# A fused layer norm, attention and token-mixing block on Trainium2: the normalised input is turned by VectorE and DMAs in place of TensorE

## The reference

```python
xn = _layernorm(x)                       # x: (8, 1024, 256), fp32
# attention: 8 query heads of 128, one shared key and value head
q  = (xn @ Wq + bq) + pe                 # Wq: (256, 1024)
k, v = split(xn @ Wkv + bkv);  k = k + pe
attn = softmax(causal(q @ k.T / sqrt(128))) @ v
attn = attn @ Wo
# token mixing
xr = mu_r * xn + (1 - mu_r) * xn_prev;   xk = mu_k * xn + (1 - mu_k) * xn_prev
ffn = sigmoid(xr @ W_r.T) * (relu(xk @ W_k.T) ** 2 @ W_v.T)
out = x + attn + ffn
```

## Time and profile before

| | us |
|---|---|
| median of 3 runs | 1504.16 (1502.83 to 1504.8) |
| the profiled execution, its own time | 1506.69 |
| its span | 1504.9 |
| PE busy | 1482.6 (99%) |
| PE weight loads busy | 1448.2 (96%) |
| DVE busy | 1268.4 (84%) |
| POOL busy | 1128.9 (75%) |
| ACT busy | 1068.0 (71%) |
| share of the chain that ended last: PE, DVE, issue, POOL | 81%, 10%, 4%, 3% |

### The profile page before, as it was taken

One profiled execution on the slowest core, in us unless ns is written; L12 is line 12 of the kernel. 1 busy time (PEld: TensorE's weight loads), 2 busy tenths in 40 slices (PEclk: granted clock), 3 DMA queues, 4 the chain that ended last, 5 costly groups with the idle time before them and its releaser, 6 DMA issues.

```text
span 1504.9 us, 36254 instructions
## 1 busy us (share of the span) xinstructions
PE 1482.6 (99%) x11724; PEld 1448.2 (96%) x11724; DVE 1268.4 (84%) x3424; ACT 1068.0 (71%) x2563; POOL 1128.9 (75%) x1541
## 2 busy tenths in 40 slices
PE   7999999999999999999999999999999999999998
PEld 7999999999999999999999999999999999999998
DVE  6999878898788987998879888798977888789885
ACT  6777667776677767767677776776767777677764
POOL 6687777777777877777777776777777787777875
PEclk8999999999999999999999999999999999999999
DMA  4144422444224442244423444134441344403453
GB/s 129 48 131 129 142 75 64 134 125 147 72 65 133 135 134 68 83 120 137 134 60 88 127 128 144 46 98 128 134 141 34 113 131 138 136 27 108 119 157 105
DMA packets 225801, 164.39 MB, mean 109 GB/s; under 512 B 51792, under 2 KB 220880, under 8 KB 225616
## 3 DMA queue, kind: packets, MB, share of 16 engines
q1 hardware_dynamic: 224768, 161.69, 35.6%
q10 hardware_dynamic: 848, 0.40, 0.1%
HBM read 81.27 MB, written 77.59 MB: 106 GB/s over the span
## 4 chain that ended last, share of the span: by engine, by line
PE 81%; DVE 10%; issue 4%; POOL 3%; DMA 1%; ACT 1%; SPq 0%; DVEq 0%; POOLq 0%; ACTq 0%
PE pS L1040 27%; PE pO L1181 22%; PE pG L1040 13%; PE pG L1127 9%; PE pT L1143 8%; DVE X L1019 2%; DVE pt L943 1%; DVE Y L923 1%; DVE kt L831 1%; POOL X L571 1%; DVE xn L808 1%; DMA park_dram<-Y 1%; DVE mix L860 1%; POOL qt L527 1%; DVE qtmp L849 1%
## 5 line engine op out<-in xcount | busy, mean ns | idle before, releaser
L764 ACT ACTIVATE X<-X,bias 128x16 f32<-128x16 f32 (+56 forms) x512 | 376.1, 734 | 150.7 <-DVE bias L1019 149.0
L1040 PE MATMUL pS<-kt,qt 128*128 128x288 f32 (+41 forms) x2304 | 460.1, 329 | 4.5 <-DVE bias L1019 3.4
L571 POOL TENSOR_SCALAR X<-X,rec 128x16 f32<-128x16 f32 (+56 forms) x512 | 378.2, 739 | 44.2 <-DVE rec L913 33.4
L1040 PEld LDWEIGHTS pS<-kt,qt 128*128 128x128 f32 x2304 | 365.7, 189 | 17.1 <-issue 5.3
L546 POOL TENSOR_TENSOR pt<-pt 128x256 fp32r<-128x256 f32 (+5 forms) x192 | 316.6, 1649 | 60.3 <-ACT pt L686 59.8
L1181 PE MATMUL pO<-pt,v 128*128 128x256 f32 x2192 | 307.6, 284 | 1.2 <-DVE ot L998 0.9
L1019 DVE CUSTOM_DVE_ANT_1 X<-pS,mask 128x528 f32<-128x528 f32 (+31 forms) x256 | 245.6, 959 | 47.1 <-PE pS L1040 42.3
L1181 PEld LDWEIGHTS pO<-pt,v 128*128 128x128 f32 x2192 | 271.9, 189 | 2.6 <-DVE ot L998 2.1
L943 DVE TENSOR_TENSOR pt<-pt,pT 128x512 fp32r<-128x512 f32 (+3 forms) x440 | 207.6, 493 | 35.1 <-ACT pt L692 32.2
L757 ACT CAST ot<-pO 128x256 fp32r<-128x256 f32 x256 | 95.5, 373 | 184.0 <-PE pO L1181 117.8
L692 ACT CAST pt<-pT 128x512 fp32r<-128x512 f32 (+3 forms) x448 | 188.0, 450 | 30.8 <-PE pT L1143 30.5
(11 more groups left out here) (120 smaller groups left out, 2298.6 us busy)
## 6 DMA issues: line engine op xcount, KB each, us to landing
park_dram<-Y SPq DMA_DIRECT2D x32, 512.0 KB, 2.6
pt<-park_dram SPq DMA_DIRECT2D x128, 128.0 KB, 2.8
park_dram<-Y SPq DMA_DIRECT2D x32, 448.0 KB, 3.0
pt<-park_dram SPq DMA_DIRECT2D x128, 112.0 KB, 2.5
park_dram<-Y SPq DMA_DIRECT2D x32, 384.0 KB, 2.9
pt<-park_dram SPq DMA_DIRECT2D x128, 96.0 KB, 2.3
park_dram<-Y SPq DMA_DIRECT2D x32, 320.0 KB, 2.7
pt<-park_dram SPq DMA_DIRECT2D x128, 80.0 KB, 2.1
```

The costliest lines, as they stand in the source:

```text
L571: nc.gpsimd.tensor_scalar(x_row(s, 0, w), x_row(s, 0, w), rec[:, j:j + 1], sign(s), ALU.mult, ALU.mult).then_inc(normed, 1)
L764: nc.scalar.activation(x_row(s, 0, w), x_row(s, 0, w), ACT.Exp, bias=bias[:, j:j + 1], scale=-1.0, accum_out=total[:, j:j + 1]).then_inc(e ...
L1040: last = nc.tensor.matmul(out, a[i], m[j], start=start and k == 0, stop=stop and k == n - 1)
```

## The change

Chunks 2 to 31 no longer go through the PE transposes of XT. DVE transposes the 32 x 32 squares of `xn` into `ka` (`turn_x`; `ka` is otherwise the activations' buffer and free at that time), SP parks `ka` in a fifth part of the DRAM buffer (`park_x`, one DMA of 256 KB) and fetches it back into `xn` with the squares in their places (`fetch_x`, four DMAs of 64 KB). ACT's two copies then read `xn` in SBUF in place of PSUM. The FK filler's activation waits until `ka` is parked (`x_parked`), `norm_apply` waits for ACT's copies (`xnt_ready`) in place of PE. `xn` is laid out by feature tile first. `MODE` becomes '0111' for rows 2 and 3: the first pair of each goes by PE. All lags, `TURNS`, `WO_AT`, `AT` and one entry of `HALVES` have new values.

```diff
--- before.py
+++ after.py
@@ -20,11 +20,11 @@
 T_LAG = 6
 PV_LAG = 8
 V_LAG = 3
-F_LAG = ((5, 2), (6, 5), (5, 5), (5, 5), (5, 6), (4, 3), (5, 5), (5, 7))
-H_LAG = ((6, 7), (9, 7), (7, 7), (7, 6), (7, 7), (7, 6), (7, 7), (7, 9))
-L_LAG = ((5, 6), (6, 7), (7, 7), (7, 9), (8, 9), (8, 11), (7, 7), (7, 8))
-W_LAG = ((7, 6), (8, 7), (7, 9), (8, 6), (7, 4), (7, 7), (7, 8), (8, 9))
-MODE = ('0000', '0000', '1111', '1111', '1111', '1111', '1111', '1111')
+F_LAG = ((4, 2), (6, 5), (5, 5), (5, 7), (4, 7), (4, 3), (5, 5), (4, 6))
+H_LAG = ((7, 7), (10, 8), (7, 8), (7, 6), (7, 9), (7, 7), (7, 7), (7, 9))
+L_LAG = ((5, 6), (7, 8), (7, 8), (8, 9), (8, 8), (7, 9), (7, 6), (7, 8))
+W_LAG = ((8, 5), (11, 5), (7, 7), (9, 6), (7, 3), (7, 5), (7, 7), (8, 9))
+MODE = ('0000', '0000', '0111', '0111', '1111', '1111', '1111', '1111')
 SCALED = ()
 C_LAG = 2
 QTMP = 4
@@ -36,10 +36,10 @@
 SHARED = NT // 2 * H
 
 
-TURNS = (((0, 'FK', 0, 0), (1, 'XT', 1, 0), (4, 'Q', 1, 0), (6, 'Q', 1, 1), (8, 'FR', 0, 0), (10, 'KV', 1, 0), (12, 'Q', 1, 2), (12, 'KT', 1, 0), (13, 'Q', 1, 3), (14, 'FV', 0, 0)), ((0, 'FK', 0, 0), (3, 'XT', 1, 0), (4, 'FR', 0, 0), (6, 'KV', 1, 0), (7, 'Q', 1, 0), (8, 'Q', 1, 1), (12, 'Q', 1, 2), (12, 'Q', 1, 3), (14, 'KT', 1, 0), (14, 'FV', 0, 0)), ((0, 'FK', 0, 0), (2, 'XT', 1, 0), (4, 'Q', 1, 0), (6, 'KV', 1, 0), (7, 'FR', 0, 0), (10, 'Q', 1, 1), (11, 'FV', 0, 0), (12, 'Q', 1, 2), (13, 'Q', 1, 3), (14, 'KT', 1, 0)), ((0, 'FK', 0, 0), (2, 'XT', 1, 0), (4, 'Q', 1, 0), (5, 'Q', 1, 1), (6, 'KV', 1, 0), (11, 'FR', 0, 0), (12, 'Q', 1, 2), (13, 'FV', 0, 0), (14, 'Q', 1, 3), (15, 'KT', 1, 0)))
-WO_AT = (17, 25, 33, 41, 49, 57, 66, 73)
-AT = {'stats': (-14, -8, -9, -7), 'apply': (-2, -1, 0, 0), 'inv': (-7, -8, -5, -6), 'mixr_prev': (0, 0, 0, 0), 'mixr_dve': (0, 0, 1, 0), 'mixr_out': (2, 1, 4, 1), 'ka_out': (4, 7, 7, 9), 'mixk_prev': (4, 8, 6, 6), 'mixk_dve': (5, 10, 6, 10), 'mixk_out': (10, 12, 10, 12)}
-HALVES = (1, 7, 6, 9, 8, 5, 1, 7, 6, 9, 8, 5, 1, 7, 6, 9, 8, 5, 1, 7, 8, 9, 1, 5, 8, 7, 1, 9, 4, 6, 5, 8, 0, 2, 4, 6, 0, 8, 4, 2, 0, 6, 4, 8, 0, 2, 4, 6, 0, 8, 4, 2, 0, 6, 4, 8, 0, 2, 4, 6, 0, 8, 4, 2)
+TURNS = (((0, 'FK', 0, 0), (1, 'XT', 1, 0), (4, 'Q', 1, 0), (5, 'Q', 1, 1), (6, 'FR', 0, 0), (12, 'Q', 1, 2), (12, 'KV', 1, 0), (12, 'Q', 1, 3), (14, 'FV', 0, 0), (15, 'KT', 1, 0)), ((0, 'FK', 0, 0), (2, 'XT', 1, 0), (4, 'FR', 0, 0), (5, 'KV', 1, 0), (7, 'Q', 1, 0), (8, 'Q', 1, 1), (12, 'Q', 1, 2), (12, 'KT', 1, 0), (14, 'Q', 1, 3), (15, 'FV', 0, 0)), ((0, 'FK', 0, 0), (2, 'XT', 1, 0), (4, 'KV', 1, 0), (6, 'FR', 0, 0), (7, 'Q', 1, 0), (10, 'Q', 1, 1), (11, 'FV', 0, 0), (12, 'Q', 1, 2), (13, 'Q', 1, 3), (14, 'KT', 1, 0)), ((0, 'FK', 0, 0), (2, 'XT', 1, 0), (4, 'Q', 1, 0), (5, 'Q', 1, 1), (6, 'Q', 1, 2), (9, 'FR', 0, 0), (10, 'KV', 1, 0), (13, 'Q', 1, 3), (15, 'FV', 0, 0), (15, 'KT', 1, 0)))
+WO_AT = (17, 26, 33, 41, 49, 56, 66, 73)
+AT = {'stats': (-14, -8, -8, -8), 'apply': (-7, -6, -7, -7), 'inv': (-9, -7, -8, -7), 'mixr_prev': (0, 0, 0, 0), 'mixr_dve': (0, 0, 1, 0), 'mixr_out': (2, 1, 4, 1), 'ka_out': (4, 6, 9, 8), 'mixk_prev': (4, 8, 6, 7), 'mixk_dve': (5, 10, 6, 9), 'mixk_out': (11, 12, 10, 14), 'xturn': (-6, -4, -5, -5), 'xfetch': (-1, -2, -3, -2)}
+HALVES = (1, 7, 6, 9, 8, 5, 1, 7, 6, 9, 8, 5, 1, 7, 6, 9, 8, 5, 1, 7, 4, 9, 1, 5, 8, 7, 1, 9, 4, 6, 5, 8, 0, 2, 4, 6, 0, 8, 4, 2, 0, 6, 4, 8, 0, 2, 4, 6, 0, 8, 4, 2, 0, 6, 4, 8, 0, 2, 4, 6, 0, 8, 4, 2)
 def fillers():
     at = {it: [] for it in range(LAST_IT)}
     for r in range(NT):
@@ -141,6 +141,11 @@
     return [1] if AT[kind][0] < 0 else []
 
 
+def by_dma(n):
+
+    return n >= 2
+
+
 def absent(b, c):
 
     return c == NC and b == B - 1
@@ -158,7 +163,8 @@
     for b, it in turns():
         if it >= T_LAG and it - T_LAG < STEPS:
             order += [(b, ("T", it - T_LAG, m)) for m in range(len(t_banks(it - T_LAG)))]
-        order += [(b, u) for u in FILL[it] if not absent(b, u[1])]
+        order += [(b, u) for u in FILL[it]
+                  if not absent(b, u[1]) and not (u[0] == "XT" and by_dma(b * NC + u[1]))]
         if SHARED <= it < STEPS:
             order.append((b, ("S", it, 0)))
     last, before = {}, {}
@@ -242,7 +248,7 @@
         mix = sb("mix", [P, CT, CHUNK])
         ka = sb("ka", [P, CT, CHUNK])
         gate = sb("gate", [P, TPC, E])
-        xn = sb("xn", [P, TPC, E])
+        xn = sb("xn", [P, CT, TPC, P])
         X = sb("X", [P, 10, T // 2])
         bias = sb("bias", [P, 10])
         total = sb("total", [P, 10])
@@ -277,6 +283,9 @@
         rstd_ready = sem("rstd_ready")
         xn_ready = sem("xn_ready")
         xnt_ready = sem("xnt_ready")
+        x_turned = sem("x_turned")
+        x_parked = sem("x_parked")
+        x_fetched = sem("x_fetched")
         xnt_zero = sem("xnt_zero")
         last_kept = sem("last_kept")
         xt_ready = sem("xt_ready")
@@ -449,6 +458,20 @@
                                  park_d[k % 4, :, q, 0:nk * 32].rearrange("(a r) n -> r a n", a=4)
                                  ).then_inc(landed[k % 4], 16)
 
+            def park_x(n):
+                sp.wait_ge(x_turned, n - 1)
+                if n > 2:
+                    sp.wait_ge(x_fetched, 64 * (n - 2))
+                sp.dma_start(park_d[4, :, :, 0:CHUNK // 2],
+                             ka[:, :, :].rearrange("p t (a n) -> p (t a) n", a=2)).then_inc(x_parked, 16)
+
+            def fetch_x(n):
+                sp.wait_ge(x_parked, 16 * (n - 1))
+                for q in range(4):
+                    sp.dma_start(xn[32 * q:32 * (q + 1), :, :, :].rearrange("r c t n -> r (c t) n"),
+                                 park_d[4, :, q, 0:CHUNK // 2].rearrange("(a r) n -> r a n", a=4)
+                                 ).then_inc(x_fetched, 16)
+
             def stack(b, c):
 
                 n = b * NC + c
@@ -466,8 +489,14 @@
                     stack(b, it // PER)
                 for s in [s for s in TURNED if s + F_LAG[s // H][s % 2] == it]:
                     fetch(b, s)
+                if it < STEPS:
+                    for n in filter(by_dma, prepared("xfetch", b, it)):
+                        fetch_x(n)
                 if it - V_LAG in TURNED:
                     park(b, it - V_LAG)
+                if it < STEPS:
+                    for n in filter(by_dma, prepared("xturn", b, it)):
+                        park_x(n)
                 for r in [r for r in range(NT) if min(WO_AT[r] + 1, LAST_IT - 1) == it]:
                     store(b, r // TPC, r % TPC)
                 for r in [r for r in range(1, NT, TPC) if min(WO_AT[r] + 4, LAST_IT - 1) == it]:
@@ -622,22 +651,27 @@
 
             def xt_out(b, c):
                 n = chunk_no(b, c)
-                act.wait_ge(filled["XT"], n + 1)
+                if by_dma(n):
+                    act.wait_ge(x_fetched, 64 * (n - 1))
+                    raw = xn[:, :, :, :].rearrange("p c t n -> p (c t n)").rearrange("p (a k j) -> p k a j", a=4, j=32)
+                else:
+                    act.wait_ge(filled["XT"], n + 1)
+                    raw = g_bank("XT", c, 0).rearrange("p (k a j) -> p k a j", a=4, j=32)
                 if n:
                     act.wait_ge(xt_ready, n)
                     act.wait_ge(prev_ready, 2 * n * CT)
                     act.wait_ge(mix_ready, 2 * n * CT)
-                g = g_bank("XT", c, 0).rearrange("p (t n) -> p t n", t=CT)
                 if c % NC:
                     nc.scalar.copy(xnt[:, :, 0:1], xnt[:, :, CHUNK:CHUNK + 1]).then_inc(last_kept, 1)
-                high = nc.scalar.copy(xt[0][:, :, :], g)
+                high = nc.scalar.copy(xt[0][:, :, :].rearrange("p c n -> p (c n)").rearrange("p (k a j) -> p k a j", a=4, j=32), raw)
                 if b is None:
                     high.then_inc(xt_first, 1)
                     weight_hi("wq1", slice(0, CT))
                     act.wait_ge(xt_ready, 1)
                 if c % NC:
                     act.wait_ge(last_kept, n - n // NC)
-                nc.scalar.copy(xnt[:, :, 1:CHUNK + 1], g).then_inc(xnt_ready, 1)
+                nc.scalar.copy(xnt[:, :, 1:CHUNK + 1].rearrange("p c (t a j) -> p c t a j", t=TPC, a=4),
+                               raw.rearrange("p (c t) a j -> p c t a j", c=CT)).then_inc(xnt_ready, 1)
 
             def kt_out(b, c):
                 act.wait_ge(kv_ready, 2 * chunk_no(b, c) + 1)
@@ -736,6 +770,8 @@
                         kt_out(b, c)
                     elif kind == "FK":
                         act.wait_ge(filled["FK"], b * NC + c + 1)
+                        if by_dma(b * NC + c + 1) and not absent(b, c + 1):
+                            act.wait_ge(x_parked, 16 * (b * NC + c))
                         nc.scalar.activation(ka[:, :, :], g_bank(kind, c, p).rearrange("p (t n) -> p t n", t=CT),
                                              ACT.Relu).then_inc(relu_ready, 1)
                         act.wait_ge(relu_ready, b * NC + c + 1)
@@ -801,13 +837,23 @@
                 nc.vector.tensor_scalar_add(vare[:, :], mv[:, :, 1], EPS).then_inc(var_ready, 1)
```

(24 more changed lines are left out.)

## The result

| | before | after |
|---|---|---|
| median, us | 1504.48 (1502.83 to 1506.9, 4 runs) | 1521.07 (1519.99 to 1522.18, 4 runs) |
| the profiled execution, its own time | 1506.69 | 1521.31 |

The ratio is 1.0108, interval 1.0095 to 1.0121: the change makes the kernel 16.6 us slower by the medians, 16.2 us by the ratio. The forecast was 1496.1, so it had the wrong direction, and its range ended at 1506.

The account below looks back on a forecast made before the run. The prediction took PE as the bound, busy for 1482.6 of 1504.9 us, with DVE second. Its terms, -13.2 - 3 + 6.1 + 2 = -8.1 us, took 1504.16 to 1496.1 us; forecast 1493 to 1500, range 1488 to 1506 us.

Parts of the forecast that it names:

- XT off PE, -13.2 - 3: On PE: 120 transposes at 0.110 us go, -13.2 us; XT's waits for the bank go too, -3 us.
- the margin of every DMA: Parks and fetches of the turned input: data there in time, every margin counted 2 us or more, cost 0.
- `MODE`, +6.1: Rows 2 and 3, first pair by PE: 56 more transposes at 0.109 us, +6.1 us; DVE's relief 0.8 us a batch.
- The timetable moves: Row 3: DVE over PE by 0.7 us a batch, 5.6 us if no lateness is forgiven; a third taken, +2 us.
- DVE becomes last in row 3: Rival: statistics, normalisation and turn in iterations 24 to 27 delay the mask; 1508 us at the full +14; chance 0.15.
- `DVE bias`: PE's wait for the mask from DVE; several times a batch in row 3 would show the forecast wrong.
- The input comes late: Rival: SP is held, the fetch lands late and ACT waits; +8 us, 1502 to 1505 us; chance 0.12.
- nothing comes of it: Rival: PE's saving becomes idle time as chains through DVE and ACT hold the length; 1502 to 1506 us; chance 0.06.
- Also the waits go: Rival: waits go too, with DVE relieved in two steps and `apply` off the crowded start; 1488 to 1491 us; chance 0.17.
- would have cost +7.7 us: The turn by the skill's rule, with DVE's time on the path: +20.9 - 13.2 = +7.7 us; not in the sum.

Follow-up runs that it names:

- e1: Changed kernel with XT of all chunks back on PE, all new orders kept: 1528.49 us, ratio 1.0155.
- e10: Kernel before with the normalisation of chunks 2 to 31 on ACT at its old places: 1508.92 us, ratio 1.0029.
- e12: e2 with the normalisation of chunks 2 to 31 on ACT: 1504.32 us, ratio 1.0003.
- e5: Kernel before with only the `AT` entries for statistics, 1/std and normalisation moved to the change's earlier places: 1516.51 us, ratio 1.0090.
- e2: Changed kernel with turn and early normalisation kept, but lags, `MODE`, `TURNS`, `WO_AT`, `HALVES` and mixing entries of before: 1525.29 us, ratio 1.0130.
- e3: Changed kernel with `MODE` of rows 2 and 3 back to '1111', nothing else: 1534.68 us, ratio 1.0193.
- e16: e12 with `MODE`, the lags of rows 2 and 3 and `HALVES` as in the change: 1496.71 us, ratio 0.9950.
- e19: Kernel before with `MODE`, the lags of rows 2 and 3 and `HALVES` as in the change: 1506.41 us, ratio 1.0014.
- e13: Changed kernel with statistics, normalisation and turn issued behind the mask of the same iteration on DVE: 1519.60 us, ratio 1.0104.
- e8: Changed kernel with filler KT of chunk 0's stretch at iteration 13 in place of 15: 1523.86 us, ratio 1.0138.
- e15: Changed kernel with `TURNS[0]` of before and nothing else: 1515.29 us, ratio 1.0073.
- e14: Changed kernel with the normalisation of chunks 2 to 31 on ACT and `TURNS[0]` of before: 1506.77 us, ratio 1.0017.
- e4: Changed kernel with DVE's turn cut to 32 of 512 columns, DMAs and waits kept, block not computed: 1518.86 us, ratio 1.0092.
- e6: Changed kernel with the normalisation written with one SBUF tensor and two columns as scalars: 1516.17 us, ratio 1.0086.

## Why the prediction was wrong

**XT off PE, -13.2 - 3.** The instructions went, the waits with them, and the margin of every DMA held: 2.6 us for the park as in the earlier trace rows, 700 ns for the turn, no wait of ACT. But the 16.2 us were never had: 7 us within the new timetable (e1 against after), about 4 with the normalisation on ACT and the old `MODE` (e10 against e12, which moves its place too), and a loss of 6 in the old timetable with the normalisation on DVE (e5 against e2). In e2 what PE no longer did turned up as waits for DVE, 18.1 us for `ot` against 11.2.

**`MODE`, +6.1.** The count was right (1304 transposes) and the sign wrong in this company. The forecast priced PE's 56 transposes in full and DVE's 0.8 us a batch, with ACT's and POOL's share, at nothing, because PE is bound on average. It is worth -12.8 us in the changed kernel (e3) and, with its lags, -8 on e12 (e16). DVE's relief in row 3, priced at nothing, is where much of it pays: from first exponent to first exponent row 3 takes 21.1 us in e3 and 20.1 in the changed kernel. In the kernel before it costs 2.1 (e19), so even there some 4 us came back. That the two terms together, -10.1, are near e16's -7.5 is therefore partly luck: neither has the size that it has in the sum, and e16 has the normalisation off DVE besides.

**"The timetable moves", priced as row 3 on DVE, +2. This is the step that failed.** Three things were wrong in it. *The duration:* it took 0.60 us for each normalisation, though the earlier trace rows showed 1.123 as the longest; at the new places it is 0.92 in the mean and up to 1.79, +20.8 us on DVE. *The place:* it looked at chunk 2's in row 3 only, and over the batches row 3 is no longer than before (20.1 against 20.4 us). Chunk 3's comes at iteration 41 in row 5, in the middle of POOL's 1.30 and 1.76 us instructions; that is where the longest wait is (7.7 us in 7 times), row 5 is 1.3 us longer a batch, and the forecast never asked what POOL would be doing in the iterations into which `apply` was moved. *The share:* it took a third of row 3's 5.6 us as if lateness were forgiven; e5 shows +13.5 us for moving statistics, 1/std and normalisation, and nothing else. How much of that is POOL's hold and how much the normalisation's mere presence there stays open (e13).

**`TURNS`, not priced at all.** The forecast named the table as changed and gave it no step. KT at 15 puts DVE's low part of `kt` just ahead of the scores that read it. It isn't all of row 1's loss: in e5, with the old fillers, row 1 takes 0.75 us more a batch than before, from exponent to exponent. The new row as a whole also empties PE in the first batch (with KT at 13, e8, the slow clock stays). Row 1 of batch 0 after, before and in e15, and then four stretches of 4 us of after, the eighth column being the granted clock:

```profile
36.00:55.10 19.10, 16.47 (x110) 15.58 (x110) 16.41 (x61) 12.42 (x44) 11.88 (x25) 0.82 0.08 23
```

```profile
35.50:50.50 15.00, 13.84 (x111) 12.78 (x109) 14.60 (x55) 11.07 (x38) 11.29 (x22) 1.00 0.01 2
```

```profile
35.90:51.30 15.40, 14.21 (x111) 12.91 (x109) 15.00 (x58) 11.30 (x38) 11.26 (x22) 1.00 0.08 24
```

```profile
36.00:40.00 4.00, 2.00 (x12) 1.60 (x13) 3.15 (x15) 3.05 (x13) 1.54 (x7) 0.93 0.00 0
40.00:44.00 4.00, 3.99 (x18) 3.70 (x19) 4.00 (x17) 3.74 (x14) 2.99 (x6) 0.50 0.01 2
44.00:48.00 4.00, 4.00 (x28) 4.00 (x27) 2.95 (x10) 0.80 (x4) 2.91 (x5) 0.71 0.02 4
48.00:52.00 4.00, 4.00 (x38) 4.00 (x37) 3.43 (x14) 2.82 (x10) 1.96 (x2) 1.00 0.13 38
```

PE was busy for 2.00 of 4 us, and then ran at 0.50 of full speed (1.2 of 2.4 GHz) through the next 4, some 4 us lost once. Both kernels have such a stretch at 28 to 32 us; in e15 the second one is not there. What the rest of the new timetable costs, `TURNS[0]` apart, the forecast put at nothing as well; with the normalisation on ACT it is 10.1 us (e14 against e16).

**The rivals.** "DVE becomes last in row 3" had part of the right mechanism, DVE late for PE by the moved normalisation, and named the row that showed it held, with a chance of 0.15 and a price of 1508; its place and its victim (`DVE bias`) were wrong, and it left row 5 and row 1 out. By the Trainium skill ("SBUF — State Buffer", Who interferes with whom) the two-input form takes the port lock and is held by GpSimd, the turn with one input is not; the trace agrees for both (up to 1793 ns against 698 to 707). "The input comes late" and "nothing comes of it" did not happen. "Also the waits go" can be said of e16 at most, whose batches 2 and 3 last 183.30 and 183.00 us. The rule of the Trainium skill ("VectorE: DVE Perf Modes", Rules for kernel authors) that would have cost +7.7 us was not what decided in the changed kernel: e4 shows the turn hidden there. In the old timetable the runs come near it, +6 from e5 to e2.

## What to carry to other kernels

A move in a timetable is priced by what the *other* engines do in the iterations that it is moved into, and by the longest duration that its line already shows, not by its mean: a line with 465 to 1123 ns for one shape is a warning. When the bound engine is relieved of work, ask which engine ends its waits next and relieve that one too; here the same saving on PE was a gain of 7 us in one timetable and a loss of 6 in another, and the kernel got faster than before only when DVE had less to do. A held instruction hides as busy time: compare the durations of a line, not only idle times. But test that the hold is what costs: in e13 it went and the time stayed.

## What the runs showed of the hardware

The normalisation as a DVE instruction with two SBUF inputs, 128 x 256 fp32, takes 0.47 us alone and up to 1.79 beside POOL's tensor instructions. Of the 64 in the changed kernel, the 16 that overlap no instruction of POOL take at most 485 ns, and the 32 that overlap a `TENSOR_TENSOR` of POOL take 660 to 1793. In the kernel before, 17 of its 19 above 600 ns overlap POOL's scaling of the probabilities (up to 1123 ns). The form with one SBUF tensor and two column scalars is held too (0.40 us to 1.66, e6), which I had not expected. The page named below counts this operation among those that can take both ports; whether it did here no run shows. Statistics on the same rows are not (their longest is 429 ns), nor is the stream transpose:

```profile
L829 DVE BATCH_NORM_STATS2 stats<-xtok x64: 406/410/429, 4.4 to 1376.3; 128x6 f32<-128x256 f32 x64
```

The Trainium skill ("SBUF — State Buffer", Who interferes with whom) gives the lock as the cause. What the runs show is durations: the long ones stand beside POOL's instructions, and the same work on ACT keeps to 586 to 603 ns. That it is the lock and not another contention between the two engines was not tested by itself.
